# One-core layer norm, attention and feed-forward kernel: the first two steps and the end laid out anew, keys packed through DRAM, and 24 identity products on TensorE at the start

## The reference

```python
xn = layernorm(x)                     # x: (16, 1024, 256) f32, no gain or bias
qkv = xn @ Wqkv.T                     # 16 heads of 16; segments of SEG = 512 tokens
q, k, v = qkv[0] * hd**-0.5, qkv[1], qkv[2]
k4, v4 = k[segment][::8], v[segment][::8]           # 64 keys for each segment
scores = q4 @ k4.T                                  # (..., 512, 64)
scores = scores.reshape(..., nb=8, BLOCK_M=64, 64)
c = max(scores, axis=block rows)                    # one for each key and block of rows
w = exp(scores - c); den = sum(w, keys) + 1e-10
att = (w @ v4) / den
h = relu(xn @ W1 + b1)                              # 256 -> 1024
return x + att @ Wout.T + h @ W2 + b2
```

## Time and profile before

| | us |
|---|---|
| median of 3 runs | 1131.93 |
| the runs | 1131.85 to 1132.47 |
| profiled execution | 1129.96 |
| its span | 1128.1 |
| TensorE busy | 1097.2 |
| VectorE / ScalarE / GpSimd busy | 742.9 / 650.4 / 620.1 |

### The profile page before, as it was taken

The page is one execution under the profiler, slowest core; times in us unless marked ns, Lnnn a source line. Parts: engine busy times, 40 slices in busy tenths (PEclk is TensorE's granted clock), DMA queues, the critical chain, the costliest instruction groups (busy, mean ns, idle before and its releaser), DMA issues.

```text
span 1128.1 us, 23167 instructions
## 1 busy us (share of the span) xinstructions
PE 1097.2 (97%) x7457; PEld 944.5 (84%) x7457; DVE 742.9 (66%) x1370; ACT 650.4 (58%) x1078; POOL 620.1 (55%) x488
## 2 busy tenths in 40 slices
PE   5799999999999999999999999999999999999997
PEld 3588988888988888988888988888988888888886
DVE  7787667657666667666667666667676667677540
ACT  4556556555656555555665556565565565555652
POOL 2435555555555555565565556466465565565464
PEclk9999999999999999999999999999999999999999
DMA  5444444344444444445344544444544353544421
GB/s 183 107 119 128 120 125 120 95 123 118 127 122 110 111 112 126 121 115 126 92 126 111 135 108 110 117 120 118 128 103 122 100 134 107 139 102 106 98 77 68
DMA packets 96139, 130.57 MB, mean 116 GB/s; under 512 B 25840, under 2 KB 54128, under 8 KB 96112
## 3 DMA queue, kind: packets, MB, share of 16 engines
q1 hardware_dynamic: 96112, 130.23, 45.2%
...
## 4 chain that ended last, share of the span: by engine, by line
PE 96%; DVE 1%; issue 1%; POOL 1%; SPq 0%; DMA 0%; POOLq 0%; ACT 0%; DVEq 0%
PE y_bank L740 40%; PE h_bank L740 40%; PE s_banks L796 5%; PE misc L866 3%; PE s_banks L866 2%; PE misc L809 2%; PE misc L740 2%; PE misc L834 0%; PE misc L817 0%; PE s_banks L740 0%; DVE w_exp L637 0%; DVE s_max L631 0%; DMA q_pack<-q_hi 0%; DVE xn_keys L592 0%; DVE w_lo L556 0%
## 5 line engine op out<-in xcount | busy, mean ns | idle before, releaser
L389 POOL TENSOR_TENSOR h_lo<-h_full,h_hi 128x512 fp32r<-128x512 f32 x256 | 336.9, 1318 | 454.5 <-ACT h_full L455 450.0
L740 PE MATMUL y_bank<-w_hi,h_hi 128*128 128x256 f32 x1024 | 290.1, 283 | 1.2 <-ACT w_exp L461 1.2
L740 PE MATMUL y_bank<-w_lo,h_hi 128*128 128x256 f32 x1024 | 289.9, 283 | 0.0
L740 PE MATMUL y_bank<-w_hi,h_lo 128*128 128x256 f32 x1024 | 289.5, 283 | 0.0
L461 ACT ACTIVATE w_exp<-w_exp 128x512 f32<-128x512 f32 x256 | 162.6, 636 | 213.7 <-DVE w_exp L637 213.7
L453 ACT ACTIVATE h_hi<-h_bank,b_cols 128x512 fp32r<-128x512 f32 x256 | 175.9, 687 | 122.5 <-PE h_bank L740 117.2
L631 DVE TENSOR_REDUCE s_max<-s_banks 128x8 f32<-128x512 f32 x256 | 175.4, 685 | 64.8 <-PE s_banks L796 63.0
L740 PE MATMUL h_bank<-xt_hi,w_hi 128*128 128x512 f32 x512 | 211.0, 412 | 1.4 <-DVE q_lo L660 1.4
L740 PEld LDWEIGHTS y_bank<-w_hi,h_hi 128*128 128x128 f32 x1024 | 195.1, 191 | 10.7 <-issue 1.4
L740 PEld LDWEIGHTS y_bank<-w_lo,h_hi 128*128 128x128 f32 x1024 | 195.4, 191 | 9.9
L740 PE MATMUL h_bank<-xt_lo,w_hi 128*128 128x512 f32 x512 | 202.4, 395 | 0.0
...
## 6 DMA issues: line engine op xcount, KB each, us to landing
q_pack<-q_hi SPq DMA_DIRECT2D x256, 128.0 KB, 2.4
x_raw<-x SPq DMA_DIRECT2D x32, 512.0 KB, 3.4
q_pack<-q_lo SPq DMA_DIRECT2D x128, 128.0 KB, 2.4
rden_rows<-rden_dram SPq DMA_DIRECT2D x128, 128.0 KB, 3.5
out<-y SPq DMA_DIRECT2D x32, 512.0 KB, 2.9
k_pack<-k_hi SPq DMA_DIRECT2D x256, 32.0 KB, 1.9
...
k_pack<-k_lo SPq DMA_DIRECT2D x128, 32.0 KB, 1.9
```

The costliest lines, as they stand in the source:

```text
L389: pool.tensor_tensor(h_part[1][:, i % HBUF], h_full[:, i % HBUF], f32(h_part[0][:, i % HBUF]), ALU.subtract).then_inc(h_lo, 1)
L740: mm = pe.matmul(ps, stationary[a], moving[b], start=start and c == 0 and n == 0, stop=stop and c == len(pairs) - 1 and n == 2, skip_group ...
```

## The change

- Start, loads: wkv before wq, each with its own semaphore; x of segment 1 before the biases, wout last.
- Start, splits: w1 and w2 are split in halves. ScalarE makes the high parts between its other work. The low parts of w1 and of the first half of w2 are made by GpSimd in `first_step`, the second half of w2 by VectorE in step -1 after the third pair, wout's by VectorE at the end of step -1. wkv's low part is made before `xn_keys`, wq's after `xkey_lo`. TensorE waits for each part where it first needs it.
- Start, TensorE: 24 products identity x identity (128x128, f32) into `y_bank[1]` before the transposes of the keys. The transposes of the first segment start per quarter of `xn` (`xn_part`). The first queries go to `y_bank`, so that the first hidden tiles need not wait for `q_lo`. `normalise(1, 1)` moves from step -1 to `first_step`, and in step -1 the transposes of x stand at i = 4 instead of 7.
- `EARLY` is 4: step -1 takes one hidden tile of segment 0 fewer, step 0 one more.
- Packing, in every step: k_hi and k_lo go to `k_dram` in two transfers, and three transfers bring them back for all pairs at once. `pack` moves q alone. TensorE waits for `k_packed` before the first scores of a step.
- Step 0: `inverse_deviation(2)` stands before `h_lo` of the last tiles of step -1, `residual(0)` after two more tiles, `invert_den` two pairs earlier.
- The last step: `att` and `att_lo` are made by VectorE (`last_attention`), `att_hi` by ScalarE before the last hidden tile, and the output is stored in two halves.

The core of the diff:

```diff
--- before.py
+++ after.py
-    EARLY = 5
+    EARLY = 4
...
-        k_pack = sb("k_pack", [P, PAIRS, P], F32R)
+        k_pack = sb("k_pack", [P, PAIRS // 2, DH, P], F32R)
+        k_dram = nc.dram_tensor("k_dram", [2, PAIRS // 2, PW, DH * P], F32).ap()
...
-                sp.dma_start(wq_raw, wq_t.rearrange("(c p) n -> p c n", p=P)).then_inc(wqkv_loaded, 16)
-                sp.dma_start(wkv_raw, wkv_t.rearrange("(c p) n -> p c n", p=P)).then_inc(wqkv_loaded, 16)
+                sp.dma_start(wkv_raw, wkv_t.rearrange("(c p) n -> p c n", p=P)).then_inc(wkv_loaded, 16)
+                sp.dma_start(wq_raw, wq_t.rearrange("(c p) n -> p c n", p=P)).then_inc(wq_loaded, 16)
                 sp.dma_start(w1_raw, w1.rearrange("(c p) n -> p c n", p=P)).then_inc(w1_loaded, 16)
                 sp.dma_start(w2_raw, w2.rearrange("(c p) n -> p c n", p=P)).then_inc(w2_loaded, 16)
+                load_x(1, 1)
+                sp.dma_start(b1_cols[:], b1).then_inc(const_loaded, 16)
+                sp.dma_start(b2_rows[:], b2.partition_broadcast(P)).then_inc(const_loaded, 16)
                 wout_heads = wout_t.rearrange("(c j a d) n -> c a j d n", c=DH, a=2, d=HD)
                 for c in range(DH):
                     for a in range(2):
 
-                        sp.dma_start(wout_raw[a::2, c], wout_heads[c, a]).then_inc(w2_loaded, 16)
-                sp.dma_start(b1_cols[:], b1).then_inc(const_loaded, 16)
-                sp.dma_start(b2_rows[:], b2.partition_broadcast(P)).then_inc(const_loaded, 16)
-                load_x(1, 1)
-                for j in range(PAIRS // 2):
+                        sp.dma_start(wout_raw[a::2, c], wout_heads[c, a]).then_inc(wout_loaded, 16)
+                keys_to_dram(-2)
+                pack(-2, 0)
+                pack_keys(-2)
...
+            def keys_to_dram(s):
+
+                sp.wait_ge(k_hi, s + 3)
+                sp.dma_start(k_dram[0].rearrange("j d n -> (j d) n"),
+                             f32(k_part[0][:]).rearrange("p c n -> p (c n)")).then_inc(k_out, 16)
+                sp.wait_ge(k_lo, s + 3)
+                sp.dma_start(k_dram[1].rearrange("j d n -> (j d) n"),
+                             f32(k_part[1][:]).rearrange("p c n -> p (c n)")).then_inc(k_out, 16)
+
+            def pack_keys(s):
+
+                sp.wait_ge(k_out, (s + 3) * 32)
+                for r, part in enumerate((0, 0, 1)):
+                    sp.dma_start(f32(k_pack[PW * r:PW * (r + 1)]).rearrange("d j c n -> d j (c n)"),
+                                 k_dram[part].rearrange("j d n -> d j n")).then_inc(k_packed, 16)
+
             def pack(s, j):
 
-                if j == 0:
-
-                    sp.wait_ge(k_hi, s + 3)
-                    sp.wait_ge(k_lo, s + 3)
-                for r, part in enumerate((0, 0, 1)):
-                    sp.dma_start(f32(k_pack[PW * r:PW * (r + 1), j::PAIRS // 2, :]),
-                                 f32(k_part[part][PW * j:PW * (j + 1)])).then_inc(pair_packed[j], 16)
...
+                    keys_to_dram(s)
                     pack(s, 0)
+                    pack_keys(s)
+                if isinstance(s, int) and s == -1:
+                    den_to_dram(s + 1)
+                if norm:
                     pack(s, 1)
-                if attention:
+                if isinstance(s, int) and s == -1:
+                    den_spread(s + 1)
+                elif attention:
                     den_to_dram(s + 1)
                 if norm:
                     pack(s, 2)
-                if attention:
+                if attention and not (isinstance(s, int) and s == -1):
                     den_spread(s + 1)
                 if norm:
                     pack(s, 3)
-                if ffn:
+                if ffn and attention:
                     sp.wait_ge(y_ready, (s + 1) * YB)
                     sp.dma_start(out_rows[s], y[:, par]).then_inc(y_stored[par], 16)
+                if ffn and not attention:
+                    for b in range(YB):
+                        sp.wait_ge(y_ready, s * YB + b + 1)
+                        sp.dma_start(out_rows[s][:, 2 * b:2 * b + 2], y[:, par, 2 * b:2 * b + 2]).then_inc(y_stored[par], 16)
...
-                    if i == 2 and attention:
+                    if i == (5 if isinstance(s, int) and s == 0 else 2) and attention:
...
+                if isinstance(s, int) and s == -1:
+                    inverse_deviation(s + 3, 1 - par)
...
+                for half in range(2):
+                    pool.wait_ge(w1_hi[half], 1)
+                    pool.tensor_tensor(w1_half(w1s[1], half), w1_half(w1_raw, half), f32(w1_half(w1s[0], half)),
+                                       ALU.subtract).then_inc(w1_lo[half], 1)
+                pool.wait_ge(w2_hi[0], 1)
+                pool.tensor_tensor(w2_half(w2s[1], 0), w2_half(w2_raw, 0), f32(w2_half(w2s[0], 0)),
+                                   ALU.subtract).then_inc(w2_lo[0], 1)
+                inverse_deviation(1, 1)
...
+                weight_hi(wkv_raw, wkv[0][:], wkv_loaded, 16, wkv_hi)
+                weight_hi(wq_raw, wq[0][:], wq_loaded, 16, wq_hi)
                 keys_hi(-2)
+                weight_hi(w1_half(w1_raw, 0), w1_half(w1s[0], 0), w1_loaded, 16, w1_hi[0])
                 transposed_hi(-2, 0)
-                split_hi(2)
+                weight_hi(w1_half(w1_raw, 1), w1_half(w1s[0], 1), w1_loaded, 16, w1_hi[1])
+                weight_hi(w2_half(w2_raw, 0), w2_half(w2s[0], 0), w2_loaded, 16, w2_hi[0])
                 queries_hi(-2, 0)
                 pair_keys_hi(-2, 0)
                 queries_hi(-2, 1)
-                for n in range(3, len(splits)):
-                    split_hi(n)
+                weight_hi(w2_half(w2_raw, 1), w2_half(w2s[0], 1), w2_loaded, 16, w2_hi[1])
                 for i in range(LAG):
                     hidden(0, i)
+                weight_hi(wout_raw, wout[0][:], wout_loaded, 64, wout_hi)
...
+                if ffn and not attention:
+                    for quad in range(QUADS):
+                        attention_hi(s, quad, par)
...
+            def last_attention(s, par):
+
+                dve.wait_ge(rden_rows_in, (s + 1) * 64)
+                dve.wait_ge(num_merged, (s + 1) * 16)
+                for quad in range(QUADS):
+                    dve.wait_ge(att_hi, (s - 1) * QUADS + quad + 1)
+                    dve.wait_ge(att_lo, (s - 1) * QUADS + quad + 1)
+                    dve.tensor_tensor(att[:, quad], num_den[:, quad, 0], rden_rows[:, quad],
+                                      ALU.mult).then_inc(att_ready, 1)
+                for quad in range(QUADS):
+                    dve.wait_ge(att_ready, s * QUADS + quad + 1)
+                    dve.wait_ge(att_hi, s * QUADS + quad + 1)
+                    dve.tensor_tensor(att_part[1][:, par, quad], att[:, quad], f32(att_part[0][:, par, quad]),
+                                      ALU.subtract).then_inc(att_lo, 1)
...
+                    if n == 1 and lead(s):
+                        dve.wait_ge(w2_lo[0], 1)
                     if attention:
                         shift_scores(s, n)
-                    if n == 1 and norm:
+                    if n == 2 and lead(s):
+                        weight_lo(w2_half(w2_raw, 1), w2_half(w2s[0], 1), w2_half(w2s[1], 1), w2_hi[1], w2_lo[1])
...
+                weight_lo(wkv_raw, wkv[0], wkv[1], wkv_hi, wkv_lo)
                 normalise_keys(0)
                 normalise(0, 0)
-                split_lo(0)
-                split_lo(1)
                 keys_lo(-2)
+                weight_lo(wq_raw, wq[0], wq[1], wq_hi, wq_lo)
                 transposed_lo(-2, 0)
                 drain_kv(-2)
-                split_lo(2)
                 mask_k(-2)
-                finish_projections(-2, 0)
-                pair_values(-2, 0)
+                queries_lo(-2, 0)
+                keys_projected_lo(-2, 0)
+                queries_lo(-2, 1)
                 statistics(1, 1)
                 statistics_done(1)
-                for w in range(3, len(splits)):
-                    split_lo(w)
                 mean_variance(1, 1)
+                pair_values(-2, 0)
+                normalise(1, 1)
...
+                    pe.wait_ge(k_packed, (s + 2) * K_PACKED)
...
+                for _ in range(24):
+                    pe.matmul(y_bank[1][:, 0:P], identity[:], identity[:], start=True, stop=True)
...
```

135 lines of the change are left out of this document (88 added, 47 removed).

## The result

The changed kernel takes 1130.58 us (median; 1128.07 to 1133.41), the kernel before, run beside it, 1132.17 (1129.64 to 1133.65). The ratio is 0.9985 [0.9978, 0.9992]: 1.6 us faster, where I had forecast 7.1, and outside my range of 1119.8 to 1128.6.

What follows compares the result with a forecast made beforehand. TensorE, busy 1097.2 of 1128.1 us, was taken as the bound, with idle and low-clock time to win at both ends. Start 3.4 plus end 3.7 made 7.1 us off the 1131.93 median: 1124.8, range 1119.8 to 1128.6.

Steps and rivals of the forecast that it cites:

- the sum of the start: Start through step 0: third scores 6.2 us earlier, less 2.8 for the moved tile, brings 3.4 us; bounds 1.0 to 6.5.
- The first segment's projections and the 24 products: Start: identity products hide under a 7.1 us wait and raise the clock; 18 products take 0.23 instead of 0.43 us.
- second rival: Start: the clock falls again between 9.8 and 11.3 us, projections 1.9 us later, 1126.7 us; chance 10%.
- Splits on GpSimd: Start: three 2.5 us GpSimd operations, the first hidden; k_lo waits 0 to 2.5 us for GpSimd, taken as 1.2.
- first rival: Start: GpSimd blocks k_lo, v's copies and xn(1) on VectorE; the start brings nothing, 1128.2 us; chance 10%.
- Packing through DRAM: Before the first scores: two transfers out, three back for all pairs; first scores at 25.0 instead of 26.3, 1.3 us won.
- Step -1: Third scores at 31.2, then VectorE is the bound for 10.5 us; k_lo at 41.8, 2.5 us earlier.
- Step 0: xn_keys by 49.8, first scores at 50.3, third scores at 51.9, which is 6.2 us earlier.
- EARLY = 4: Puts one hidden tile back behind the third scores of step 0, 2.8 us that TensorE still has to do.
- The steady loop: Same TensorE work, 6 SP issues fewer per step; k_packed has 0.9 to 2.0 us of cover, so no effect.
- The end: Last segment: the 3.3 us wait for att_lo goes, the halved store gives 0.4; 3.7 us, bounds 3.3 to 4.1.
- The sum: Whole kernel: 3.4 + 3.7 = 7.1 us off the median, 1124.8 us; the ends give 1121.3 to 1127.6.

Runs made afterwards that it cites:

- klo_first: The changed kernel, but GpSimd starts the low part of w2's first half only when VectorE's k_lo is done; 1128.41 us, ratio 0.9972.
- no24: The changed kernel without the 24 identity products on TensorE at the start; 1130.32 us, ratio 0.9986.
- best4: early5_klo_bridge with k packed from SBUF instead of through DRAM; 1123.60 us, ratio 0.9926.
- early5_unpacked: The changed kernel with EARLY = 5 and k packed from SBUF, pair group by pair group, as before; 1126.14 us, ratio 0.9946.
- before_again: The kernel before, unchanged, profiled and timed again; 1132.76 us, ratio 1.0006.
- before_early4: The kernel before with EARLY = 4 in place of 5 and nothing else; 1134.12 us, ratio 1.0016.
- early5: The changed kernel with EARLY = 5 in place of 4; 1124.85 us, ratio 0.9944.
- end_alone: The kernel before with only the new end: last att and att_lo on VectorE, earlier att_hi, store in halves; 1126.65 us, ratio 0.9957.
- early5_klo: The changed kernel with EARLY = 5 and GpSimd's low part of w2's first half waiting for k_lo; 1123.22 us, ratio 0.9927.
- early5_klo_bridge: early5_klo with 24 more identity products on TensorE ahead of the first scores of step -1; 1123.65 us, ratio 0.9928.
- res2: The changed kernel with x_b of step 0 on GpSimd back at its old place, before the later tiles' h_lo; 1127.65 us, ratio 0.9963.

## Why the prediction was wrong, point by point

What failed is the sum of the start, "6.2 - 2.8 = 3.4 us": it lost 4.3 in the profiles. In it failed the wait of k_lo at the start, the gain of the packing, the queries of step -1 at the high clock, the third scores of step 0 without a wait for their q, and EARLY = 4 at the tile's own time. The chain of the start by the steps of the forecast (us):

| | forecast | after | klo_first | before |
|---|---|---|---|---|
| k_lo ends | 18.3 | 19.4 | 17.5 | 20.3 |
| first scores | 25.0 | 26.3 | 24.8 | 26.3 |
| third scores | 31.2 | 33.4 | 31.1 | 32.6 |
| k_lo of step -1 starts | 41.8 | 45.1 | 42.3 | 44.3 |
| q_lo ends | 44.3 | 49.9 | 46.9 | 46.8 |
| first scores, step 0 | 50.3 | 55.8 | 52.9 | 52.3 |
| third scores, step 0 | 51.9 | 58.5 | 55.5 | 58.1 |

- **The first segment's projections and the 24 products**: right in their sizes (0.39 us products from 11.8), but the 24 products are worth nothing in the sum, as no24 shows. I had priced the low clock by one profile, in which it rose at 17.2; in the four others with the old start it rose at 14.5 to 16.6, and in no24 at 14.4. In the profile of best4 the second rival (the clock falls again) came true, in spite of the 24 products. I had also let the gain run through to the scores; the transfers and GpSimd's rival work lay behind it.
- **Splits on GpSimd**: "I take 1.2, the middle" failed. k_lo was held for 2.0 us, within 0.5 of my bad end, because GpSimd, busy with the first two until 16.8, goes straight on to the third 0.3 us before k_lo's turn. The exclusion that the Trainium skill (SBUF — State Buffer, Who interferes with whom) states is what the trace shows: 2.38 us beside GpSimd, 0.41 once GpSimd waits. By it the same holds for the half of w2 in step -1 (2.25 us for 1.22, beside an h_lo on GpSimd from 35.02 to 36.30), which I had put down at 1.22. Taking the first of these away gives 2.2 us of median (1.7 by the means). The first rival (GpSimd blocks VectorE, 1128.2) had the mechanism at 10%, and a start that brings nothing where this one lost 4.3.
- **Packing through DRAM**: "1.3 us won here" failed. Alone it costs 3.0 us of v1 and 1.3 of median (the interval of its ratio begins at 1.0000); beside the other edits it is level. Before the first scores stand eight issues instead of six, and the round trip begins with k_lo. My 25.0 was right only where k_lo is not held (24.8 in klo_first), and early5_unpacked reaches 24.95 without the round trip, with k_lo held: the gain was the earlier k_lo, not the packing.
- **Step -1**: the forecast had "after that VectorE is the bound", and then left 2.5 us from k_lo to the end of q_lo, the distance of before (44.28 to 46.82), where the queries stood 0.23 apart. A bounding VectorE means idle TensorE, 2.24, 2.11 and 0.72 us here, and my own reading of the earlier trace rows was that such a gap brings the low level back. From k_lo to the end of q_lo it took 4.75 us, not 2.5. This 2.3 is the largest error of a single row of the table. No run keeps the clock high there and changes nothing else, so its price in time is not shown; before_again has the same happen within one kernel.
- **Step 0**: "6.2 earlier" is 0.4 later. Of the 6.6 us between, 1.3 are there at the first scores (k_lo, 1.1, and the landing), 0.9 by the third (low clock), 1.1 by k_lo of step -1 (the half of w2), 2.3 by q_lo, 1.0 at the third scores of step 0. The shares of one profile are no surer than the spread said above. The last one has a cause that I had not seen. SP of the changed kernel, between the first scores' operands and the third's:

```profile
51.85 1.54 SPq L331 DMA_DIRECT2D k_pack<-k_dram  x3
53.44 1.16 SPq L348 DMA_DIRECT2D den_dram<-num_den  x2
...
56.00 0.59 SPq L341 DMA_DIRECT2D q_pack<-q_hi  x1
```

  The q of the second pair group is issued behind the k reads and, since `den_to_dram` was moved in front of it in step -1, behind two more issues; the last of it, issued at 56.00, lands in 2.4 us, at 58.4. The forecast's own figures (q_lo at 44.3, eleven issues 0.64 apart, 2.4 to land) give 53.1 for it, not 51.9. All eleven profiles with the new start end this wait with q_pack (1.0 to 3.4 us idle), none with the old start does. No run moves `den_to_dram` back, so what that is worth is open.
- **EARLY = 4** was sized at 2.8; the tile alone is that in the profile (2.75 in before_early4; by the median that kernel lost 1.8). But in step -1 the tile lay in idle time: with it the queries start at 42.57, without it at 43.20. early5 against after: 0.9 at the third scores, 3.0 for the tile, and 1.3 for a wait that I had not seen at all, x_b behind the moved tile's h_lo and in front of rden_rows; 5.1 of v1, 5.7 of median (4.1 by the means). Not one of the seven profiles with EARLY = 4 has its queries of step -1 all at the high clock (3.6 to 4.8 us from the first to the last); of the nine with EARLY = 5 four have (2.5 to 2.6), the others 3.9 to 4.7. Three of these four have the old start, so with the new one it is none of six against one of five: that the missing tile makes the low clock there likelier is not shown, and what decides it is open.
- **The steady loop**: right. k_pack<-k_dram lands in 2.7 us at the median (forecast 2.4 to 3.5), and TensorE never waits for it between 60 and 1089 us.
- **The end**: the wait of 3.3 is gone and the tail is 4.0 shorter in the profiles (the store in halves lands 1.0 sooner: 256 KB in 2.0 us, 512 KB in 3.0). Against the median the term was too small. The wait can be followed by the low clock, in four profiles not at all (37.9, 38.0), for a part of the product (39.3) or for all of it (40.4); with the new end the tail is 33.8 to 33.9 in eleven of twelve (34.9 in early5_unpacked, which waits 1.0 us for h_lo). end_alone took 5.8 us off.
- **The sum**: in the profiles the start is 7.7 us worse than forecast (-4.3 for 3.4): 6.6 at the third scores of step 0 and 1.3 for the wait behind x_b, less 0.2. In medians the end is 2.1 better (5.8 for 3.7). Together 5.6, where 5.5 are missing (1.6 for 7.1). So the end covers what the start lost, and 2.1 us of that are luck: I had sized it from an execution of the rarer kind. Over end_alone the changed kernel loses 3.9 us by the medians. EARLY = 5 takes that back, and whether the rest of the start then wins anything is not shown by early5 (1.8 by the medians, 0.6 by the means), but is by early5_klo (3.4 and 2.6, with all five runs below all six of end_alone).

The best version here, early5_klo, undoes EARLY and lets GpSimd wait for k_lo: 1123.22 us, some 9 under the kernel before and 7.4 under the changed one. The two variants of it (early5_klo_bridge and best4) are level with it. It was not run with x_b at its old place (res2) or with `den_to_dram` behind the second group of q.
